# The next group's x split and two quantisation slabs moved in a transformer layer on eight cores

## The reference

```python
def _kernel_exp(x):
    return jnp.exp(x - jnp.max(x, axis=-1, keepdims=True))
q, k, v = proj(Wq, bq), proj(Wk, bk), proj(Wv, bv)      # x @ W.T + b, split in heads
q_kern, k_kern = _kernel_exp(q), _kernel_exp(k)
kv = jnp.einsum('bhsd,bhse->bhde', k_kern, v)
k_sum = jnp.sum(k_kern, axis=2)
denom = jnp.einsum('bhqd,bhd->bhq', q_kern, k_sum) + 1e-06
y = jnp.einsum('bhqd,bhde->bhqe', q_kern, kv) / denom[..., None]
x = _layernorm(x + (y.reshape(b, s, e) @ Wo.T + bo))

def _quantize(W):
    gamma = jnp.mean(jnp.abs(W))
    return jnp.clip(jnp.round(W / (gamma + EPS)), -1.0, 1.0)
h = jax.nn.relu(x @ _quantize(W1).T + b1)
x = _layernorm(x + (h @ _quantize(W2).T + b2))
```

## Time and profile before

| | us |
|---|---|
| median of 3 runs (3733.5 to 3808.9) | 3734.49 |
| profiled execution | 3730.12 |
| its span, slowest core (0) | 3728.6 |
| spans of the eight cores | 3719.5 to 3728.6 |
| PE busy | 3359.9 |
| one step of phase 2 (start of the last L950 of an FFN to the next: 2648.02 to 2829) | 181 |

### The profile page before, as it was taken

The page is one execution under the profiler, slowest core; times in us unless marked ns, Lnnn a source line. Parts: engine busy times, 40 slices in busy tenths (PEclk is TensorE's granted clock), DMA queues, the critical chain, the costliest instruction groups (busy, mean ns, idle before and its releaser), DMA issues.

```text
span 3728.6 us, 54018 instructions; the slowest of 8 cores (3719.5 to 3728.6 us)
## 1 busy us (share of the span) xinstructions
PE 3359.9 (90%) x19971; PEld 1983.8 (53%) x19971; DVE 1333.2 (36%) x1871; ACT 948.8 (25%) x1665; POOL 121.6 (3%) x253
## 2 busy tenths in 40 slices
PE   4999989988989898989898898989898989898987
PEld 1445444444646464646565555556464646464655
DVE  4564466653232323242323232323232323232221
ACT  2110000002223232222323232223232323232332
POOL 0000010000000000000000000000000000000000
PEclk9999999998999999999999999999999999999999
DMA  5553255541515142424243333333242424242424
GB/s 180 158 158 113 88 167 170 169 131 60 159 56 163 60 156 69 146 77 145 83 133 100 125 108 111 113 102 122 94 132 84 139 77 150 66 157 64 162 80 133
DMA packets 247425, 443.45 MB, mean 119 GB/s; under 512 B 22640, under 2 KB 88192, under 8 KB 247168
## 3 DMA queue, kind: packets, MB, share of 16 engines
q1 hardware_dynamic: 226688, 370.24, 32.0%
q0 software_dynamic: 20480, 69.75, 5.3%
HBM read 406.34 MB, written 33.56 MB: 118 GB/s over the span
## 4 chain that ended last, share of the span: by engine, by line
PE 79%; DVE 9%; ACT 5%; DMA 3%; issue 3%; DVEq 0%; ACTq 0%; POOL 0%; SPq 0%; POOLq 0%
PE p L950 22%; PE p L1000 11%; PE p L1016 9%; PE p L285 4%; PE p L288 4%; PE p L291 4%; PE p L294 4%; PE p L297 4%; PE p L305 3%; PE p L853 2%; DMA wsl<-w1r 2%; PE p L896 1%; PE p L890 1%; PE p L899 1%; PE p L893 1%
## 5 line engine op out<-in xcount | busy, mean ns | idle before, releaser
L1028 DVE SCALAR_TENSOR_TENSOR hl<-h,hh 128x256 bf16<-128x256 f32 x512 | 217.6, 425 | 1216.9 <-ACT h L1024 1208.4
L950 PE MATMUL p<-w2s,hh 128*128 128x512 bf16 x2048 | 609.0, 379 | 24.6 <-DVE hl L1028 24.4
L950 PE MATMUL p<-w2s,hl 128*128 128x512 bf16 x2048 | 609.0, 379 | 0.0
L1000 PE MATMUL p<-x1Th,w1s 128*128 128x256 bf16 x4096 | 533.7, 273 | 8.7 <-ACT x1Th L750 7.2
L1021 ACT ACTIVATE hh<-p,b_c 128x256 bf16<-128x256 f32 x512 | 242.8, 474 | 997.6 <-PE p L1011 991.7
L1000 PEld LDWEIGHTS p<-x1Th,w1s 128*128 128x128 bf16 x4096 | 398.5, 98 | 164.9 <-issue 17.3
L1016 PE MATMUL p<-x1Tl,w1s 128*128 128x256 bf16 x3584 | 477.3, 273 | 3.2 <-DVE x1Tl L756 3.1
L1016 PEld LDWEIGHTS p<-x1Tl,w1s 128*128 128x128 bf16 x3584 | 348.6, 98 | 50.3 <-issue 10.3
L950 PEld LDWEIGHTS p<-w2s,hl 128*128 128x128 bf16 x2048 | 200.1, 98 | 241.8
L950 PEld LDWEIGHTS p<-w2s,hh 128*128 128x128 bf16 x2048 | 196.1, 98 | 174.8 <-issue 43.7
L1024 ACT ACTIVATE h<-p,b_c 128x256 f32<-128x256 f32 x512 | 242.7, 474 | 48.2 <-ACT hh L1021 1.1
(11 more groups left out here) (155 smaller groups left out, 4512.6 us busy)
## 6 DMA issues: line engine op xcount, KB each, us to landing
w1s<-w1q SPq DMA_DIRECT2D x467, 256.0 KB, 3.2
w2s<-w2q SPq DMA_DIRECT2D x467, 256.0 KB, 2.8
xg<-xfm SPq DMA_DIRECT2D x64, 512.0 KB, 6.3
wsl<-w1r SPq DMA_DIRECT2D x64, 512.0 KB, 4.4
wsl<-w2r SPq DMA_DIRECT2D x64, 512.0 KB, 4.4
xt<-xtm SPq DMA_DIRECT2D x32, 512.0 KB, 3.5
out<-ot POOLq DMA_DIRECT2D x32, 512.0 KB, 4.5
w1s<-w1q POOLq DMA_DIRECT2D x45, 256.0 KB, 3.2
```

Of the source, the lines that this page charges most:

```text
L950: stf=stf, spf=spf: e.matmul(PB[4 + 2 * ti + nci][:, 0:512], hbuf[:, ti * 128:(ti + 1) * 128], w2s[wb][:, nci * 512:(nci + 1) * 512], star ...
L1000: e.matmul(hp[:, 0:TG * 128], w1s[wb][:, fc, :], x1Th[par][:, fc, :], start=(fc == 0), stop=False), waits=w)
L1028: e.scalar_tensor_tensor(hl[cb][:], h32[cb][:], 1.0, hh[cb][:], op0=OP.mult, op1=OP.subtract), waits=((sS, e_h32),))
```

## The change

In the step of phase 2 the two `load_x_tile` calls for the next group are emitted before `emit_attn_rest` instead of after it; the two `load_xt` calls stay behind it. In phase 1 of the second sequence the 64 quantisation slabs are distributed differently: two instead of four directly behind the sequence boundary, five instead of four before tiles 1 and 2, four before each later tile as it was.

```diff
@@ phase 1, loop over tiles @@
             elif not (si == 1 and i == 0):
-                for _ in range(4):
+                for _ in range(5 if i in (1, 2) else 4):
                     emit_quant_slab()
...
             if si == 1 and i == 0:
                 emit_seq_boundary(0)
-                for _ in range(4):
+                for _ in range(2):
                     emit_quant_slab()
@@ phase 2, loop over groups @@
-        emit_attn_rest(si, gi)
         if idx + 1 < len(groups):
             nsi, ngi = groups[idx + 1]
             load_x_tile(nsi, ngi * TG + 0)
             load_x_tile(nsi, ngi * TG + 1)
+        emit_attn_rest(si, gi)
+        if idx + 1 < len(groups):
+            nsi, ngi = groups[idx + 1]
             load_xt(nsi, ngi, 0)
             load_xt(nsi, ngi, 1)
         emit_x1tr(si, gi, tis=(0,))
```

## The result

| | before | changed |
|---|---|---|
| median of 10 executions, us | 3734.08 | 3530.95 |
| ratio, with its 95% interval | | 0.9448 (0.9433 to 0.9464) |
| spans of the eight cores in the profiled execution, us | 3719.5 to 3728.6 | 3514.8 to 3527.4 |
| mean granted clock | 0.964 to 0.966 | 0.989 to 0.992 |
| PE busy | 90% | 94% |

By the medians the kernel became 203 us faster, by the ratio 206; 201 had been worked out. In some executions on all eight cores one die, sometimes both, has a lower clock than otherwise (0.81 on core 2 of e3_one_tile from 60 to 510 us): these are left out of every ratio here but not out of the medians, and where a profile was hit, only the cores of the other die are read.

A forecast was written before the change was run, and what follows sets the result against it. PE's order of work, busy 90%, was taken as the bound; 162.7 (wait) + 36 (clock) - 1.3 (first group) + 3.6 (slabs) = 201 us off, so 3533 us, ratio 0.946. Range 3520 to 3548; 8 times in 10, 3512 to 3572.

The forecast's parts named there:

- the wait of 162.7 us: L285, first Q projection matmul, waits for DVE's xgl in 15 steps; the whole 162.7 us was to be won.
- ACT's hole: ACT idle 5.39 us before L835; the 2.21 us split pair fits with 2 us to spare, cost 0.
- DVE's 0.4 us: DVE's 2.56 us xgl pair before L869 delays the yTl by 0.4 us, hidden from PE, cost 0 to 0.1.
- the order on SP: SP's DMA queue keeps its order xg, xg, xt, xt, as emit_attn_rest issues no DMA.
- Rival A: Attention tail delayed by both pairs, 4.8 us a step, 72 us: 3605 us, with half of it 3569; chance 0.07.
- The clock term: Slow matmuls behind the pause before the Q projection vanish: 15 x 2.41 = 36 us won.
- The second view of the prediction: Q matmuls' mean of 409 against 379 ns: some 182 slow matmuls at 0.211 us extra spacing, 38 us.
- Rival B: Pause before the Q projection goes, slow stretch stays, so only the wait is won: 3569 us; chance 0.07.
- The first group: No FFN in front, so DVE's 2.56 us pair delays yTl and L853; cost 0 to 2.6, 1.3 us taken.
- The slabs: Phase 1, second sequence: tile 1's evacuation 4.5 us earlier, some given back one tile on; 3.6 us won, bounds 0 and 4.5.
- Rival C: ACT stands at L262 waiting for xg, the 10.8 us idle time only changes places: about 3730 us; chance 0.03.
- rival D: Output and Q projections without a pause run at the lower clock, 40 us more a step: 4130 us; chance 0.03.

The follow-up runs named there:

- e3_one_tile: Changed kernel with only the first tile's x split ahead of the attention tail, the second's behind; no ratio, spans of cores 4 to 7 3530.3 to 3537.9 us.
- e1_split_only: Kernel before with only the next group's x split moved ahead of the attention tail, slabs as they were; ratio 0.9472, median 3533.8 us.
- e3b_one_tile: Changed kernel with only the first tile's x split ahead of the attention tail, the second's behind, run again; ratio 0.9502, median 3548.2 us.
- e5_low_twice: Changed kernel with each of the two xgl instructions of a phase 2 step done twice on DVE; ratio 0.9602, median 3582.7 us.
- e4_fill_pause: Kernel before with 46 extra matmuls filling the pause before the Q projection, wait for xgl left in; ratio 0.9929, median 3705.6 us.
- e9_low_behind: Changed kernel with other PSUM banks in the attention tail and DVE's low parts of the split behind both tiles' yTl; ratio 0.9360.

## Why the prediction was right

**The bound and its cause.** That PE's order is the path and that the wait of 162.7 us lay in the queues of ACT and DVE held in full. e1_split_only has the gain, and e3b_one_tile, in which only the place of one split is different, has a wait of the size that was worked out for it.

**What is hidden.** ACT's hole (it was left with 2.96 us), DVE's 0.4 us (0.46) and the order on SP came out to a tenth of a microsecond or so. Rival A, which charged part or all of the pair to the tail, did not occur; e5_low_twice shows the price that it would have had, and that it was near: 2.56 us more of DVE work in each step cost 52 us. The estimate of rival A, 72 us for both pairs of 4.8 us in each step, left out the falls of the clock that came with such a wait in e5_low_twice; no run shows what it would have been.

**The clock term.** 36 us was somewhat too small. Counted over each Q projection of core 0, from the first start to the last against 95 distances of 0.216 us, the slow matmuls took 38.5 us before (2.0 to 2.8 us a step) and nothing after; the five other cores whose first Q matmul is recorded give 36.3 to 37.5. The pause in front of them, from the last transpose to L285, shrank from 11.1 to 0.1 us, 165 us in 15 steps where the recorded idle time is 162.7. Together with the first group, 1.6 us to the bad (below), that is the 202 us of the 15 steps. The second view of the prediction, by the mean length, had given 38, and e4_fill_pause gives about the same. The mistake was to choose the smaller of two sizes: the prediction's own reading of one step, 5.07 - 2.59 = 2.48 us for twelve matmuls, is already more than the 2.41 that its product uses. Rival B (the slow stretch stays) did not occur in the changed kernel; but the runs show that it was nearer than its reasoning said: in e3b_one_tile and e4_fill_pause the clock did fall at the small gaps behind the FFN, in a third of the steps, and in the changed kernel itself in 4 of 15 steps on core 5, which is why its steps took 2438.1 us.

**The first group.** 1.3 us was charged to DVE's pair. The cost came, by another way. ACT and PE on core 0 of the changed kernel:

```profile
831.81 2.21 ACT L262 ACTIVATE xgh<-xg 128x1024 bf16<-128x1024 f32 x2
834.11 1.29 ACT L835 ACTIVATE qb<-p 128x512 f32<-128x512 f32 x2
...
834.85 3.75 PE L853 MATMUL p<-qb,kv 128*128 128x128 f32 x16 [4.90 <-ACT qb L835]
```

ACT, too, has no hole there, and its pair kept L853 waiting for 4.90 us instead of 2.60. The output projection started 48.0 us after the first Q matmuls (842.09 - 794.12) instead of 46.4 (849.72 - 803.34), 1.6 us later. The step named only DVE and should have named both engines.

**The slabs.** 3.6 us was forecast, the bounds 0 and 4.5. The means over the cores show about 5 and the slowest core none; the wait for `kkern` at its place fell from 13.0 to 4.9 us on core 0 and from 10.9 to 8.5 on core 2. The size is within what the cores differ by anyway, so it can be called neither right nor wrong for the measured time. That the whole came out within a few us is in part chance: the pause and the clock were 5 us too small together, and the slabs gave less on the core that set the time.

**The signs named beforehand.** No wait of L285 for `xgl`; a step of 167.3 us on core 0 ((3346.35 - 1003.94) / 14, between starts of L853) for the 168 forecast; Q matmuls of 379 ns; a mean clock of 0.99. Rival C (the idle time only changes places) and rival D (the denser stretch lowers the clock) did not occur, as the same lines show: L262 waited 0.22 us for x, and the projections behind one another ran at 0.38 us a matmul, at a granted clock of 1.00 from 2524 to 2567 us. The rule of the Trainium skill named with rival D, a peak-current limiter under dense load on three or more cores of a die, did not show in the compared executions: PE was busy 94% of the time on all eight cores at a clock of 0.99. But the 0.81 named in the section on the result has just the value of the page's 13/16, so the prediction went too far in setting the rule aside by one trace. What brings this level about was not tried.

## What to carry to other kernels

Where PE waits for a small preparation of the next stage, look for where that instruction stands in its engine's queue before looking at its cost or its transfer; give each engine's part the place where that engine has a hole (here ACT's before the tail, DVE's behind the critical evacuations), and leave the DMAs where no urgent load is queued behind them. Price a pause of PE with what comes after it: here the slow stretch added 2.5 us to 11, and where DVE kept PE waiting behind the FFN, falls of the clock added some 9 us to 39. To shorten a pause to a few microseconds was not to win the clock back: 3.9 us still lost it nearly every time, and 0.9 us kept it.

## What the hardware showed that was not expected

A pause of 3.9 us brought TensorE to its lower level (0.50 in the window behind it) just as one of 10.8 us did, in 117 of 120 steps; one of 0.9 us between large matmuls did not. The Trainium skill (TensorE: Matmul & The Clock Gate, Part 1, HAM oscillation) describes such a loss at every pause of a loop; the trace of the kernel before agrees, with 1.5 us or more of slow matmuls behind each of the 15 pauses on every core. Behind the FFN, where small f32 transposes and products with gaps of 1.88, 0.6 and 0.7 us follow one another, the clock fell in some steps and not in others, with the same instructions: on core 0 in 1 of 15 steps of the kernels before and after, 5 of e3b_one_tile, 6 of e4_fill_pause. Each fall cost 1.4 to 1.6 us in the last two. They are not scattered: on all eight cores of these two kernels, 4 to 6 of the 15 steps have one, mostly two or three steps apart. What decides it from step to step was not tried; the kernels differ in the length of a step (180.9, 167.3, 168.5, 178.8 us), and that this plays a part is only a guess. With the wait for DVE's evacuation gone (e9_low_behind) seven of eight cores had no fall at all.
